# Attention outputs: the multiplication by the inverse denominators and the lower halves on VectorE instead of GpSimd

## The reference

```python
# x: (2, 2048, 512); 16 heads of 32
def _L0_attn_ref(x, Wqkv, Wout, bout):
    qkv = x @ Wqkv.T
    q, k, v = jnp.split(qkv, 3, axis=-1)
    q, k, v = map(merge_heads, (q, k, v))
    dots = jnp.einsum('bhid,bhjd->bhij', q, k) * dh ** (-0.5)
    dots = jnp.where(causal_mask, -jnp.inf, dots)
    attn = jax.nn.softmax(dots, axis=-1)
    out = jnp.einsum('bhij,bhjd->bhid', attn, v)
    return out.transpose(0, 2, 1, 3).reshape(b, t, d) @ Wout.T + bout
...
x = _layernorm(x + attention(x))
x = _layernorm(x + cross_attention(x, ctx_1024))
x = _layernorm(x + experts(x))
```

## Time and profile before

| | |
|---|---|
| median of 3 runs | 2635.22 us |
| span of the profiled execution | 2629.2 us |
| the median less that span | 6.0 us |
| attention, about | from 300 to 1360 us of the span |

### The profile page before, as it was taken

How to read it: one execution, slowest core, us unless ns; L and a number is a source line. 1 busy time by engine, 2 the same in 40 slices (tenths; PEclk the granted TensorE clock), 3 DMA queues, 4 the chain that set the end, 5 groups by cost and what they waited for, 6 DMA issues and landing times. The chain is left out here.

```text
span 2629.2 us, 42902 instructions
## 1 busy us (share of the span) xinstructions
PE 2430.0 (92%) x13556; PEld 1018.3 (39%) x13556; DVE 1715.9 (65%) x3957; ACT 1097.3 (42%) x2066; POOL 1119.8 (43%) x404
## 2 busy tenths in 40 slices
PE   8999799999999999999956799999999999999998
PEld 3444223332333233323213354444445454454543
DVE  4443687776777677767405477767677776767665
ACT  4331256665666566666623242332324232322420
POOL 0000379988898989898952111102111111101100
PEclk9999799999999999999977899999999999999999
DMA  7864312212121212140021101010100101010000
GB/s 250 294 212 156 89 38 54 58 42 59 42 58 42 63 38 76 28 111 20 25 93 60 45 1 62 1 46 18 41 22 1 63 1 46 17 45 17 1 17 17
DMA packets 130506, 155.66 MB, mean 59 GB/s; under 512 B 19838, under 2 KB 98174, under 8 KB 129245
## 3 DMA queue, kind: packets, MB, share of 16 engines
q1 hardware_dynamic: 130269, 152.69, 18.9%
HBM read 99.96 MB, written 52.17 MB: 58 GB/s over the span
## 5 line engine op out<-in xcount | busy, mean ns | idle before, releaser
L762 ACT ACTIVATE probs<-st_ps 128x512 f32<-128x512 f32 (+3 forms) x1280 | 605.3, 536 | 359.0 <-PE st_ps L865 206.6
L637 POOL TENSOR_TENSOR total<-total,probs 128x2048 f32<-128x2048 f32 (+3 forms) x200 | 706.3, 3531 | 77.8 <-ACT probs L762 65.6
L804 DVE TENSOR_REDUCE seg_max<-s_ps 128x1 f32<-128x512 f32 x768 | 506.2, 684 | 143.4 <-PE s_ps L851 139.9
L865 PE MATMUL st_ps<-q_pair,k_pair 98*128 98x512 f16 (+3 forms) x1280 | 445.5, 362 | 36.6 <-ACT probs L762 22.7
L851 PE MATMUL s_ps<-k_pair,q_pair 96*128 96x512 f16 (+3 forms) x1280 | 446.0, 363 | 31.9 <-DMA q_pair<-q_parts 11.2
L1429 PE MATMUL fps<-x2T,w_p_hi 128*128 128x512 f16 x1024 | 317.3, 379 | 0.0
L885 PE MATMUL o_ps<-probs,v_sb 128*32 128x512 f32 (+3 forms) x2560 | 309.0, 556 | 0.0
L808 DVE CUSTOM_DVE_ANT_0 s_ps<-s_ps,later 128x384 f32<-128x384 f32 (+3 forms) x512 | 250.4, 497 | 89.1 <-issue 85.9
L1429 PE MATMUL fps<-w_p_hi,hT 128*128 128x512 f16 x1024 | 306.1, 381 | 0.0
L865 PEld LDWEIGHTS st_ps<-q_pair,k_pair 98*128 98x128 f16 x1280 | 124.8, 99 | 357.7 <-ACT probs L762 264.7
L1133 POOL TENSOR_TENSOR rstd<-rstd,keep_power 128x4 f32<-128x4 f32 x24 | 26.1, 1090 | 552.0 <-DVE rstd L1254 552.0
(11 more groups left out here) (164 smaller groups left out, 3403.8 us busy)
## 6 DMA issues: line engine op xcount, KB each, us to landing
k_pair<-k_parts SPq DMA_DIRECT2D x96, 128.0 KB, 3.6
q_pair<-q_parts SPq DMA_DIRECT2D x96, 128.0 KB, 4.7
x_raw<-xT_in SPq DMA_DIRECT2D x8, 1024.0 KB, 6.3
q_parts<-qk_out SPq DMA_DIRECT2D x32, 256.0 KB, 3.6
k_parts<-qk_out SPq DMA_DIRECT2D x32, 256.0 KB, 3.9
piece_raw<-w_in SPq DMA_DIRECT2D x8, 1024.0 KB, 8.7
v_rows<-v_out SPq DMA_DIRECT2D x32, 256.0 KB, 2.2
w_parts<-piece_cut SPq DMA_DIRECT2D x8, 1024.0 KB, 5.6
```

What stands on the lines that cost most here:

```text
L637: last = nc.gpsimd.tensor_tensor(summed[:, :, off:], other[:, :, off:], probs[:, k % NP, :, off:], ALU.add)
L762: nc.scalar.activation(probs[:, k % NP, h, off:], st_ps[:, p % (2 * NVU) % RING, off:], ACT.Exp, scale=SCALE).then_inc(exp_done.sem, 1)
L804: nc.vector.reduce_max(highest, s_ps[:, slot], AX.X).then_inc(s_read.sem, 1)
L865: last = nc.tensor.matmul(st_ps[:, slot, off:], k_pair[a][:, h, kt * P:(kt + 1) * P], q_pair[a][:, c, h, off:], start=True, stop=not diagonal)
```

## The change

Both operations, 128x512 elements each, leave GpSimd's program and enter VectorE's, at the same lags 38 and 49 and with the same waits. In VectorE's `step` they stand behind that unit's maxima. The two semaphore counts `scaled` and `split_done` are started by VectorE. `schedule()` now counts 0.6 of VectorE time at each of the two units, so that the table of maxima moves.

```diff
--- before.py
+++ after.py
@@ -458,6 +458,8 @@
         busy = [0.0] * NVU
         for t in LAST_TILE:
             busy[(t * HG + HG - 1 + INVERTED) % NVU] += 0.2
+            for lag in (SCALED, LOWER):
+                busy[(t * HG + HG - 1 + lag) % NVU] += 0.6
         cost = []
         for what, c, unit in AUX:
             if what == "rows":
@@ -616,8 +618,6 @@
             nc.gpsimd.memset(k_pair[1][NR:NM], QK).then_inc(factors_ready, 1)
             pool.wait_ge(factors_ready, 2)
             added.lead(pool)
-            scaled.lead(pool)
-            split_done.lead(pool)
 
             def step(i, s, first, end):
                 k = tile_at(s, 1, first, end)
@@ -639,18 +639,6 @@
                     if starts and off:
                         last = nc.gpsimd.tensor_copy(summed[:, :, 0:off], other[:, :, 0:off])
                     last.then_inc(added.sem, 1)
-                c = chunk_at(s, SCALED, first, end)
-                if c is not None:
-
-                    pool.wait_ge(inv_loaded[c % 2], 16 * (CPB * i + c // 2 + 1))
-                    pool.wait_ge(split_done.sem, split_done.at(i, c - 1))
-                    nc.gpsimd.tensor_tensor(o_sb[:], o_raw[:, c % 2], inv[:, c % 2],
-                                            ALU.mult).then_inc(scaled.sem, 1)
-                c = chunk_at(s, LOWER, first, end)
-                if c is not None:
-                    pool.wait_ge(o_hi_done.sem, o_hi_done.at(i, c))
-                    nc.gpsimd.tensor_tensor(o_out[:, c % 2, 1], o_sb[:], o_out[:, c % 2, 0],
-                                            ALU.subtract).then_inc(split_done.sem, 1)
 
             laps(pool, step)
 
@@ -783,7 +771,7 @@
 
         @block.vector
         def _(dve):
-            for count in (s_read, max_ready, recips):
+            for count in (s_read, max_ready, recips, scaled, split_done):
                 count.lead(dve)
 
             def aux(i, n):
@@ -820,6 +808,17 @@
                 if c is not None:
                     dve.wait_ge(den_moved[c % 2], 16 * (CPB * i + c // 2 + 1))
                     nc.vector.reciprocal(inv_small[:, c % 2], inv_small[:, c % 2]).then_inc(recips.sem, 1)
+                c = chunk_at(s, SCALED, first, end)
+                if c is not None:
+                    dve.wait_ge(inv_loaded[c % 2], 16 * (CPB * i + c // 2 + 1))
+                    dve.wait_ge(split_done.sem, split_done.at(i, c - 1))
+                    nc.vector.tensor_tensor(o_sb[:], o_raw[:, c % 2], inv[:, c % 2],
+                                            ALU.mult).then_inc(scaled.sem, 1)
+                c = chunk_at(s, LOWER, first, end)
+                if c is not None:
+                    dve.wait_ge(o_hi_done.sem, o_hi_done.at(i, c))
+                    nc.vector.tensor_tensor(o_out[:, c % 2, 1], o_sb[:], o_out[:, c % 2, 0],
+                                            ALU.subtract).then_inc(split_done.sem, 1)
 
             dve.wait_ge(made, 7)
             for n in range(AHEAD):
```

## The result

The changed kernel takes 2674.02 us (median of 4 runs, 2671.99 to 2680.65), the kernel before 2635.14 us on the same chip. The ratio is 1.0149, interval 1.0135 to 1.0164: slower by 39 us. The span of the profiled execution went from 2629.2 to 2671.9 us. Attention ends 36.8 us later (the second half's first product starts at 1400.6 instead of 1363.8 us).

A forecast was written before the change was run, and what follows sets the result against it. TensorE was taken as the bound. Terms -45.4 - 3.4 + 56 + 32 = +39 us on the span of 2629.2 gave 2668, with 6.0 us to the median 2674; likeliest case 2645 to 2712, 8 in 10 within 2615 to 2725.

The forecast's parts named there:

- The mechanism: On VectorE, a moved operation waits for the rest of GpSimd's running addition, then takes 0.54 us; up to 5.1 us.
- The gain that was taken away: Second chunks' ends: ScalarE's wait behind GpSimd's multiplication goes, 21.6 us idle plus 23.8 us clock; 3.4 us at attention's end.
- The 3.4 us at attention's end: Attention's end: two moved operations leave GpSimd's additions, 2.4 us; the very last multiplication and subtraction get shorter, 1.0 us.
- The four places: Four places in each group where VectorE meets an addition and TensorE stalls: 8.0 us, seven times, 56 us.
- fourth chunk, lower half: VectorE has just caught up and meets the next additions: loss about 1.5 us, an estimate.
- The two close places: First chunk's lower half and second chunk's multiplication, expected about 0.2 and some 0.5 us ahead of an addition, costing nothing.
- the second rival: The two close places meet additions: 18 + 25 = 43 us, clock up to another 45; 2717 to 2762, chance 0.20.
- The clock: TensorE's half-speed stretches after new stalls above 2 us: fourteen times 3.4 us is 48, two thirds counted, 32 us.
- The table: The changed table of maxima moves some products by a unit or two; nothing set, VectorE's 27% idle time covers it.
- The first rival: Waits stay within three score buffers, or the moved table gives VectorE more room; only the gain remains: 2586 to 2605, chance 0.19.
- the three buffers: Score buffers that let TensorE be only three products ahead of the maxima; the first rival had them hold the waits.

The follow-up runs named there:

- later upper half: Kernel before the change with the upper half at lag 50 in place of 46, lower half, store and tail 4 units later: 2596.03 us, ratio 0.9857.
- after: The changed kernel, with multiplication and lower half moved from GpSimd to VectorE, against the kernel before: 2674.02 us, ratio 1.0149.
- the run with other places: Changed kernel with the fourth chunk's multiplication 5 units later, second and third chunks' lower halves 3 and 2 later: 2631.59 us, ratio 0.9990 to the kernel before.
- the run with one input: Changed kernel with both moved operations reading one SBUF tensor, multiplication and subtraction left out: 2596.00 us, ratio 0.9854 to the kernel before.

## Why the prediction was right, point by point

The time was predicted as 2674 us and measured as 2674.02. Direction and mechanism are shown. The sizes of the terms are not all as predicted, errors cancel, and that the two times agree so closely is luck.

**The mechanism: right.** "VectorE waited for the whole rest of GpSimd's operation and then did its work", read from one line of the second half, with 0.54 us behind it. In attention it is 0.55 us in all 46 cases. Reading one input removes the waits, shorter additions halve the longest. The prediction's row for VectorE coming in between two GpSimd operations, L1380, is itself a case of waiting: 0.95 us, where its shortest takes 0.41.

**The gain that was taken away, 45.4 + 3.4 us: too large.** The later upper half takes most of ScalarE's wait away without moving any work and gives 38.2 us (2634.26 to 2596.03). In the profiles attention is 37.0 us shorter with it: 15.8 us less idle time and 21.2 us less busy time of TensorE for the same products (946.0 to 924.8). The prediction had 21.6 and 23.8. Its windows count all of TensorE's idle time in 85 us and not the stalls alone, and they charge the clock for the idle part of a window as well. The 3.4 us at attention's end hardly came: the wait for the last addition went from 11.54 to 10.92 us and the next gap from 16.10 to 15.15, but a new one of 1.81 us stands at 1336.2.

**The four places, 8.0 us: 7.2 measured.** Seven times each, as predicted:

| place | predicted | TensorE's stall after |
|---|---|---|
| fourth chunk, multiplication | 2.6 | 2.59 to 2.74 |
| fourth chunk, lower half | 1.5 | about 0.3 |
| second chunk, lower half | 2.5 | 2.94 to 3.47 |
| third chunk, lower half | 1.4 | 1.04 to 1.06 |

The sum of the seven groups is 51 us, predicted 56. The weakest term was the one without a row, the fourth chunk's lower half; in the run with other places it stays at its lag and turns dear, 2.02 to 2.11 us. The two close places fell as forecast: the first chunk's lower half ends ahead of an addition (0.68 us), the second chunk's multiplication passes between two (1.07 us), so the second rival did not come. It was not far off: with the lower half alone on VectorE the first chunk's does meet nearly a whole addition, 2.2 to 2.5 us of stall in each of eight groups, where the rival had some 2.2.

**The clock, 32 us: about 25.** Against the run with one input TensorE's busy time rises by 25.1 us, with 64.8 us more at 1.2 GHz. The share of two thirds was a choice; about half of its 48 us came. The traces do not show why one stall is followed by 3.4 us at 1.2 GHz and another by 6.8.

**The table, nothing: wrong.** "VectorE's idle time of 27% covers the shift" failed. Alone the table costs 9.7 to 12 us, and with the waits of after it saves 28.6. It is no neutral shift but a second change, which here belongs to the first.

**The sum came out** because a gain put 12 us too high meets losses put 14 us too high. In the profiles attention is 37.1 us shorter with one input than before, where 48.8 were predicted; the waits add 48.7 us of idle time and 25.1 of busy time, where 56 and 32 were predicted. That makes 36.7 us, against 39. The second half's 5.9 us, for no reason of the change, are no part of the prediction.

**The first rival** (2586 to 2605) has the time that the chip gave when the second SBUF input was taken away, 2596, but not for the rival's reason: the three buffers did not hold the waits.

## What to carry to other kernels

When an engine stands waiting for a slow one, first ask how much later the waiter may come: one lag of 4 units gave 38 us here, where moving the work cost 39. Before an elementwise operation with two SBUF inputs goes to VectorE, look at what GpSimd does at that place: its price is the rest of GpSimd's instruction and 0.55 us, not its own 0.68, and everything behind it on VectorE pays. If it has to stand there, cut GpSimd's instructions shorter or have VectorE read one input from PSUM, as the diagonal maxima do here (not tried for these two operations), and follow each moved operation through SP's queue as well.

## What the runs showed that was not expected

- A table that only moves the same maxima by a unit or two costs 9.7 us with the operations on GpSimd, nothing with two short ones on VectorE, and saves 28.6 us with two long ones.
- Mending three places out of eight made a fourth one about seven times as dear (0.3 to 2.02 us).
- The time at 1.2 GHz in the second half, whose program is the same in all kernels, ran from 92.0 to 108.2 us between the profiles, and its length from 1265.3 to 1271.2 us: as much as some of the effects that were to be told apart in attention.
